# dt and u in the order of the units: one 512 KB spread with 4 KB pieces in place of two with 2 KB pieces

## The chip, the cores and the metric

The kernel runs on one core of a Trainium2 chip, in one launch. The metric is the device time of that launch in microseconds (us); lower is better. A core has TensorE (PE; its weight loads are listed as PEld), VectorE (DVE), ScalarE (ACT), GpSimd (POOL) and SyncE (SP), which run their own instruction streams and wait for each other on semaphores, and 16 DMA engines that move data between the memories. In this kernel SP alone issues DMAs.

## The reference

A layer over an input of 8 x 512 x 256: causal latent attention with 16 heads, a feed-forward part with blockwise 4-bit rounding, a two-directional state-space model, and the feed-forward part again, each with a residual. The change is in the state-space model. For each of the 8 batch elements and 2 directions it computes, with 512 channels, 16 states and 512 time steps:

```
dt  = softplus(dt @ dt_w + dt_b)                    # 512 steps x 512 channels
dA  = exp(dt[..., None] * A)                        # A: 512 channels x 16 states
dBu = dt[..., None] * B_ssm[:, :, None, :] * xc[..., None]
def step(h, inp):
    dAt, dBut, ct = inp
    h = dAt * h + dBut
    return h, einsum('bdn,bn->bd', h, ct)
y = scan(step, 0, (dA, dBu, C_ssm)) + xc * D_skip
```

u is dt * xc; dBu is u times the row of B of each state.

## The kernel before

**Blocks, groups, units.** Each batch element is a block of 64 units, numbered K = 0 to 511 over the kernel (NU = 64, NK = 512). A group g is 128 channels in one direction; a block has 8 groups, and a group has 8 units (q = 0 to 7). A unit is 16 channels with all 16 states, as two halves e = 0 and 1 of 8 channels x 16 states = 128 partitions x 512 steps.

**A unit's work.** ACT makes the factors dA of both halves (`factors`, L1355) into two PSUM banks; POOL makes dBu of both halves in one instruction (`make_dBu`, L1074); DVE scans each half (L943) and multiplies it by C (L950); PE sums the states of two units at a time (`state_sum`, L1657). There is one pair of factor banks, so ACT waits for DVE's L950 of the unit before. dBu has four slots; the dBu of unit K+2 stands before unit K's other work on POOL, and waits until the pair before it was summed. In the last block the odd units from k = 15 (`shared`) have their second half multiplied by POOL (L1081).

**How dt and u come to 128 partitions.** dt and u of a group are 128 channels x 512 steps in SBUF. SP stores each to DRAM (`store_dt`, `store_u`: `kept_dt[g]`, `kept_u[g]`, 128 rows of 2 KB), and for each unit loads the 8 rows of a half, repeated for the 16 states, to 128 partitions: a spread of 256 KB, twice for a unit and tensor (`spread_dt`, L581; `spread_u`, L572). The rows of a half are

```
def row_block(q, e):
    return QG * ((2 * q + e) % QG) + q // 2        # QG = 4
r = CT * row_block(q, e)                           # CT = 8
return kept[r:r + CT].unsqueeze(0).to_broadcast([DS, CT, T])
```

so the two halves of a unit lie 32 rows apart. u has two buffers (US = 2), dt has three (RS = 3).

**The order on SP.** In unit K the queue has: the spread of dt for K+3 (after dA of K), the spread of u for K+4 (after dBu of K+2), behind q = 0 the load of the next xc, behind q = 3 the stores of the next group's dt and u, behind q = 6 the load of the next dt input, and four units before a new direction the rows of B and C (`load_states`, L588 and L592). The first spread of a group waits for that group's store (L577, L568). A waiting instruction holds all that stands behind it on SP.

**The side work.** Between the units each engine does visits of the work beside: the merge, the output and the second feed-forward part of the block before (`merge`, 18 visits, and `ffn`, 47), and latents (26), attention (65), the first feed-forward part (47) and the preparation (`prep`, 27) of the block after. How many visits stand at each half unit is written out by hand in `VISITS`, one base-36 digit for each half unit, and all engines follow the same table: "first" for block 0, "middle" for blocks 1 to 6, "last" for block 7.

## Time and profile before

| | us |
|---|---|
| median of 3 runs (3790.64 to 3798.03) | 3791.13 |
| profiled execution, its own time | 3796.87 |
| its span | 3795.1 |
| DVE busy | 3057.4 |
| PE busy | 2855.8 |
| ACT, POOL busy | 1991.5, 1949.1 |

The profiled execution's time is 1.8 us more than its span, and 5.7 us above the median. The span divides into about 317 us ahead of the first unit, 402 us for block 0, about 442 us for each of the blocks 1 to 6, 331 us for block 7 and 93 us behind the last unit. The busy shares are means over stretches that are limited by different things, so they say little of themselves: it has to be read where an engine is nearly always busy, and what it waits for where it is not.

### The profile page before, as it was taken

The page shows a single profiled execution, that of the slowest core. Times are in us where ns is not written, and L with a number is a line of the kernel's source. Part 1 is how long each engine was busy: PE and PEld are TensorE (multiplying, and loading weights), DVE is VectorE, ACT ScalarE, POOL GpSimd, SP SyncE. Part 2 cuts the span into 40 slices and gives each one's busy share as a digit, 9 for nine tenths or more (in the row PEclk, how much of TensorE's full clock was granted, in tenths as well). Part 3 has the DMA queues.
Part 4 walks back from the last instruction along what each step waited for, and adds up shares of the span by engine and source line. Part 5 has one row for each costly group of instructions (what it writes and reads, how often), then busy time and mean ns, then how long its engine had stood idle before and what let it go on. Part 6 is the DMA issues. An engine that isn't in the chain of part 4 may idle for free.

```text
span 3795.1 us, 41535 instructions
## 1 busy us (share of the span) xinstructions
PE 2855.8 (75%) x12965; PEld 1467.3 (39%) x12965; DVE 3057.4 (81%) x4262; ACT 1991.5 (52%) x3811; POOL 1949.1 (51%) x1115
## 2 busy tenths in 40 slices
PE   7963877689776987679776897769866797765436
PEld 3631444245423553245442454235532454422103
DVE  5354889797988989788897979888897888979765
ACT  2533665446653575546654466535755466544332
POOL 2014754556545654447545565456544475456671
PEclk9976988899987998799988999879987999887657
DMA  3007885966668665867759666786658677597890
GB/s 94 1 17 209 212 221 159 273 159 179 175 205 240 174 179 152 252 166 193 206 150 272 160 177 175 204 240 175 180 153 247 168 192 208 144 269 209 233 246 19
DMA packets 373277, 691.40 MB, mean 182 GB/s; under 512 B 52157, under 2 KB 63552, under 8 KB 366912
## 3 DMA queue, kind: packets, MB, share of 16 engines
q1 hardware_dynamic: 373056, 688.74, 67.3%
q8 instruction: 104, 1.70, 0.2%
q14 instruction: 117, 0.96, 0.1%
HBM read 603.65 MB, written 84.93 MB: 181 GB/s over the span
## 4 chain that ended last, share of the span: by engine, by line
PE 42%; DVE 27%; ACT 9%; issue 7%; POOL 7%; DMA 6%; SPq 1%; POOLq 0%; ACTq 0%; DVEq 0%
PE banks L1387 22%; DVE banks L943 7%; PE banks L1579 5%; PE banks L1392 5%; POOL sb_arena L1074 4%; DVE sb_arena L950 4%; PE banks L1657 4%; PE banks L1555 3%; ACT banks L1355 3%; ACT sb_arena L1121 2%; DMA sb_arena<-kept_u 2%; PE banks L1427 2%; DVE sb_arena L652 2%; PE banks L1401 2%; DVE sb_arena L847 2%
## 5 line engine op out<-in xcount | busy, mean ns | idle before, releaser
L1074 POOL TENSOR_TENSOR sb_arena<-sb_arena 128x1024 f32<-128x1024 f32 x512 | 1205.6, 2359 | 970.3 <-PE banks L1657 605.5
L943 DVE TENSOR_TENSOR_SCAN banks<-banks,sb_arena 128x512 f32<-128x512 f32 x999 | 1171.4, 1217 | 277.0 <-ACT banks L1355 203.5
L1355 ACT ACTIVATE banks<-sb_arena,sb_neg_a 128x512 f32<-128x512 f32 x1024 | 665.1, 682 | 982.8 <-DVE sb_arena L950 792.0
L1657 PE MATMUL banks<-sb_arena,sb_w_sum 128*32 128x512 f32 x2048 | 336.5, 729 | 461.7 <-DVE sb_arena L950 363.4
L950 DVE TENSOR_TENSOR sb_arena<-banks,sb_arena 128x512 f32<-128x512 f32 x999 | 636.8, 678 | 0.0
L1392 PE MATMUL banks<-sb_ident,sb_arena 128*128 128x128 f32 (+1 forms) x2083 | 358.5, 296 | 364.3 <-POOL sb_arena L984 153.2
L1121 ACT ACTIVATE sb_arena<-banks 128x512 f32<-128x512 f32 (+2 forms) x720 | 360.6, 517 | 510.7 <-PE banks L1392 344.8
L1392 PEld LDWEIGHTS banks<-sb_ident,sb_arena 128*128 128x128 f32 (+1 forms) x2083 | 242.4, 148 | 575.0 <-ACT sb_arena L1121 224.4
L801 DVE TENSOR_REDUCE sb_nmax<-banks 128x1 f32<-128x512 f32 (+3 forms) x352 | 222.7, 635 | 187.0 <-PE banks L1582 186.5
L1387 PE MATMUL banks<-sb_w_gu,sb_arena 128*128 128x352 f32 x1024 | 362.5, 505 | 5.5 <-ACT sb_arena L1121 5.5
L1579 PE MATMUL banks<-sb_arena 128*128 128x384 f32 (+3 forms) x1024 | 361.1, 464 | 4.5 <-POOL sb_arena L1001 4.5
L1657 PEld LDWEIGHTS banks<-sb_arena,sb_w_sum 128*32 128x32 f32 x2048 | 46.0, 117 | 633.1 <-DVE sb_arena L950 443.6
L991 POOL TENSOR_TENSOR sb_arena<-sb_arena,sb_q_s 128x704 f32<-128x704 f32 x64 | 88.7, 1386 | 377.1 <-DVE sb_arena L670 367.5
L1197 ACT ACTIVATE sb_arena<-banks,sb_nmax 128x512 f32<-128x512 f32 (+3 forms) x512 | 266.2, 536 | 26.4 <-DVE sb_nmax L801 25.7
L1387 PEld LDWEIGHTS banks<-sb_w_gu,sb_arena 128*128 128x128 f32 x1024 | 209.0, 212 | 119.9 <-issue 31.5
L1387 PE MATMUL banks<-sb_arena,sb_w_lat 128*128 128x512 f32 x512 | 233.8, 607 | 13.3 <-DVE sb_arena L788 8.2
L1427 PE MATMUL banks<-sb_arena,sb_w_merge 128*128 128x512 f32 x448 | 215.4, 640 | 0.0
L1401 PE MATMUL banks<-sb_identb,sb_zerob 128*128 128x512 bf16 x640 | 215.1, 411 | 0.0
L1387 PE MATMUL banks<-sb_w_down,sb_arena 128*128 128x256 f32 (+1 forms) x768 | 205.1, 412 | 9.6 <-ACT sb_arena L1121 7.8
L1555 PE MATMUL banks<-sb_arena 128*32 128x128 f32 x2560 | 185.9, 280 | 1.9 <-ACT sb_arena L1121 1.9
L1387 PE MATMUL banks<-sb_arena,sb_w_in 128*128 128x512 f32 x256 | 151.0, 725 | 47.8 <-DVE sb_arena L847 46.9
L1579 PEld LDWEIGHTS banks<-sb_arena 128*128 128x128 f32 x1024 | 156.0, 194 | 66.4 <-issue 43.3
(132 smaller groups left out, 4020.9 us busy)
## 6 DMA issues: line engine op xcount, KB each, us to landing
sb_arena<-kept_dt SPq DMA_DIRECT2D x1024, 256.0 KB, 5.2
sb_arena<-kept_u SPq DMA_DIRECT2D x1024, 256.0 KB, 4.6
kept_xc<-sb_arena SPq DMA_DIRECT2D x16, 1024.0 KB, 4.9
kept_z<-sb_arena SPq DMA_DIRECT2D x16, 1024.0 KB, 5.5
sb_arena<-kept_xc SPq DMA_DIRECT2D x64, 256.0 KB, 5.6
kept_dt<-sb_arena SPq DMA_DIRECT2D x64, 256.0 KB, 3.9
kept_u<-sb_arena SPq DMA_DIRECT2D x64, 256.0 KB, 3.9
sb_arena<-kept_z SPq DMA_DIRECT2D x63, 256.0 KB, 5.8
```

The costliest lines, as they stand in the source:

```text
L943: v.tensor_tensor_scan(products if e == 1 and shared(K) else factors, factors, products, 0.0, ALU.mult, ALU.add).then_inc(V.sem, V.mark("s ...
L950: v.tensor_tensor(dBu[K % SLOTS][:, e], psum[:, e], ct[:, gd % 2], ALU.mult).then_inc(V.sem, V.mark("hc", K, e))
L1074: nc.gpsimd.tensor_tensor(dBu[K % SLOTS], rows_u[K % US], bt[:, gd % 2].unsqueeze(1).to_broadcast([P, 2, T]), ALU.mult).then_inc(G.sem, G. ...
L1121: nc.scalar.activation(dst, src, ACT.Copy).then_inc(A.sem, A.mark(*name))
L1355: nc.scalar.activation(psum[:, e], rows_dt[K % RS][:, e], ACT.Exp, scale=neg_a[:, s, m, j:j + 1]).then_inc(A.sem, A.mark("dA", K, e))
L1387: mm = pe.matmul(dst, lhs, rhs, start=(i == 0), stop=(i == len(pairs) - 1))
L1392: mm = pe.transpose(dst, src, ident[0:src.shape[0], 0:src.shape[0]])
L1401: pe.matmul(psum[:, YB], zerob[:, :], identb[:, :].unsqueeze(1).to_broadcast([P, T // P, P]), start=False, stop=False)
L1427: mm = pe.matmul(psum[:, SB[j]], w_merge[:, k, j * P:j * P + P], ycat[:, k], start=(k == 0), stop=(k == 2 * DT - 1))
L1555: mm = pe.matmul(psum[L * r:L * r + L, SB[4], m * P:m * P + P], val[:, at:at + L], prT[:, slot, c * P:c * P + P], start=(k == 0), stop=(k ...
L1579: pe.matmul(psum[:, bank, e * kl:e * kl + kl], qz[:, m, r], lat[1][:, m, 0:kl], start=(e == 0), stop=False)
L1657: mm = pe.matmul(psum[r:r + L, YB], w_sum[:, L * o:L * o + L], dBu[k % SLOTS][:, e], start=(o == 0), stop=(o == QG - 1))
```

## The change

The two DRAM tensors get the shape (group, unit of the group, channel of the half, half, step): 16 rows of 2 KB of one unit lie together, and a channel's two halves are 4 KB in a row. Each group's store is cut by blocks of 32 partitions, four for dt and four for u, each writing 32 pieces of 2 KB. Each unit's spread is one DMA for both halves. The counts in the waits follow. `VISITS` has other numbers; the visits in sum, and the instructions of PE, DVE, ACT and POOL, are the same.

```
@@ VISITS (of three tables, the first row of "middle") @@
-    "middle": "0012003103011116093755733052020212123201040107405110222120313130"
+    "middle": "1112010202101035082933111352315112022111201302010323102032211031"
...
-        kept_dt, kept_u = scratch("kept_dt", (NG, P, T)), scratch("kept_u", (NG, P, T))
+        kept_dt, kept_u = scratch("kept_dt", (NG, NQ, CT, 2, T)), scratch("kept_u", (NG, NQ, CT, 2, T))
...
             def store_u(g):
                 sp.wait_ge(G.sem, G.at("u", g))
-                sp.dma_start(kept_u[g], u).then_inc(s_kept_u, 16)
+                for r in range(QG):
+                    sp.dma_start(blocks_of(kept_u[g], r), u[L * r:L * r + L]).then_inc(s_kept_u, 16)
+
+            def blocks_of(kept, r):
+
+                return kept[r // 2::2, :, r % 2]
+
+            def over_states(kept, q):
+
+                return kept[q].rearrange("c e t -> c (e t)").unsqueeze(0).to_broadcast([DS, CT, 2 * T])
 
             def spread_u(K):
                 g, q = divmod(K, NQ)
                 if q == 0:
-                    sp.wait_ge(s_kept_u, 16 * (g + 1))
+                    sp.wait_ge(s_kept_u, 16 * QG * (g + 1))
                 if K >= US:
                     sp.wait_ge(G.sem, G.at("dBu", K - US))
-                for e in range(2):
-                    sp.dma_start(rows_u[K % US][:, e], over_states(kept_u[g], q, e)).then_inc(s_u[K % US], 16)
+                sp.dma_start(rows_u[K % US].rearrange("p e t -> p (e t)"), over_states(kept_u[g], q)
+                             ).then_inc(s_u[K % US], 16)
```

`store_dt` and `spread_dt` change in the same way.

How SP's queue changes is seen at a store, here that of the second group (the names: `kept_dt` and `kept_u` are the DRAM tensors, `sb_arena` holds the buffers). Before:

```order
L581 DMA sb_arena<-kept_dt 128x1x512 x2
L572 DMA sb_arena<-kept_u 128x1x512 x2
L554 DMA kept_dt<-sb_arena 128x512
L558 DMA kept_u<-sb_arena 128x512
L581 DMA sb_arena<-kept_dt 128x1x512 x2
L572 DMA sb_arena<-kept_u 128x1x512 x2
```

And now:

```order
L585 DMA sb_arena<-kept_dt 128x1x1024
L576 DMA sb_arena<-kept_u 128x1x1024
L555 DMA kept_dt<-sb_arena 4x8x512 x4
L560 DMA kept_u<-sb_arena 4x8x512 x4
L585 DMA sb_arena<-kept_dt 128x1x1024
L576 DMA sb_arena<-kept_u 128x1x1024
```

A spread went from two issues to one, a pair of stores from two issues to eight, and the DRAM side of a store now has an outer dimension of 4.

What the table moves is seen on DVE in block 3, at the units k = 33 to 35, which lie in attention (L801, now L806, is attention's maximum; L943 and L950, now L948 and L955, are a unit's scan and its product with C). Before:

```order
L943 SCALAR_TENSOR_TENSOR banks<-banks,sb_arena 128x512 x2
L801 TENSOR_REDUCE sb_nmax<-banks 128x1
L950 TENSOR_TENSOR sb_arena<-banks,sb_arena 128x512 x2
L943 SCALAR_TENSOR_TENSOR banks<-banks,sb_arena 128x512 x2
L801 TENSOR_REDUCE sb_nmax<-banks 128x1
L950 TENSOR_TENSOR sb_arena<-banks,sb_arena 128x512 x2
L943 SCALAR_TENSOR_TENSOR banks<-banks,sb_arena 128x512 x2
L807 TENSOR_TENSOR sb_arena<-sb_arena,banks 128x512
L801 TENSOR_REDUCE sb_nmax<-banks 128x1
L950 TENSOR_TENSOR sb_arena<-banks,sb_arena 128x512 x2
```

And now:

```order
L948 SCALAR_TENSOR_TENSOR banks<-banks,sb_arena 128x512 x2
L806 TENSOR_REDUCE sb_nmax<-banks 128x1
L955 TENSOR_TENSOR sb_arena<-banks,sb_arena 128x512 x2
L817 TENSOR_TENSOR sb_x<-sb_xin,banks 128x256
L806 TENSOR_REDUCE sb_nmax<-banks 128x1
L678 BN_STATS sb_stats<-sb_x 128x6
L806 TENSOR_REDUCE sb_nmax<-banks 128x1 x5
L948 SCALAR_TENSOR_TENSOR banks<-banks,sb_arena 128x512 x2
L806 TENSOR_REDUCE sb_nmax<-banks 128x1 x3
L826 RECIPROCAL sb_einv<-sb_esum 128x16
L806 TENSOR_REDUCE sb_nmax<-banks 128x1 x5
L955 TENSOR_TENSOR sb_arena<-banks,sb_arena 128x512 x2
```

Attention's steps were spread over the units one at a time; now more than a dozen of them stand within two units, and fewer units stand between attention's beginning and its end (16.5 in place of 19 in a middle block, counted from the tables).

## Rows read from the trace of the kernel before

**Rows 1.** The page: shares of the chain that ended last, by engine.

```profile
PE 42%; DVE 27%; ACT 9%; issue 7%; POOL 7%; DMA 6%; SPq 1%; POOLq 0%; ACTq 0%; DVEq 0%
```

**Rows 2.** Stretches: us; PE, PEld, DVE, ACT, POOL busy; PEclk, DMA share, GB/s.

```profile
1603.00:1627.00 24.00, 20.97 (x50) 8.42 (x50) 18.86 (x30) 9.34 (x15) 13.15 (x7) 0.93 1.07 272
...
1645.00:1705.00 60.00, 44.81 (x174) 26.83 (x172) 53.83 (x86) 28.32 (x42) 25.45 (x17) 0.89 0.44 119
...
1744.00:1775.00 31.00, 30.40 (x181) 18.81 (x179) 22.40 (x30) 19.88 (x66) 24.32 (x13) 1.00 0.72 184
...
2010.00:2027.00 17.00, 4.42 (x20) 0.61 (x18) 14.37 (x18) 9.53 (x17) 9.65 (x6) 0.67 1.03 278
2027.00:2047.00 20.00, 7.04 (x26) 1.40 (x27) 14.47 (x17) 5.42 (x9) 12.80 (x7) 0.50 0.98 283
```

**Rows 3.** The chain, start us, us, what: the edge between blocks 4 and 5.

```profile
2460.49 5.53 DMA sb_arena<-kept_u
...
2476.40 4.90 DMA kept_u<-sb_arena
...
2481.87 0.60 SPq L572
...
2482.57 4.13 DMA sb_arena<-rows_bc
...
2499.20 0.60 SPq L572
...
2500.73 7.67 DMA sb_arena<-kept_zs
```

**Rows 4.** The timeline of that edge: in brackets the engine's idle time and its releaser.

```profile
2490.10 1.30 ACT L1355 ACTIVATE banks<-sb_arena,sb_neg_a 128x512 f32<-128x512 f32 x2 [6.00 <-DMA sb_arena<-kept_dt]
...
2490.89 2.35 DVE L943 TENSOR_TENSOR_SCAN banks<-banks,sb_arena 128x512 f32<-128x512 f32 x2 [3.78 <-ACT banks L1355]
...
2493.15 1.27 DVE L950 TENSOR_TENSOR sb_arena<-banks,sb_arena 128x512 f32<-128x512 f32 x2
```

**Rows 5.** The timeline in block 7, two units, POOL and PE.

```profile
3603.11 2.34 POOL L1074 TENSOR_TENSOR sb_arena<-sb_arena 128x1024 f32<-128x1024 f32 x1 [1.79 <-DMA sb_arena<-kept_u]
...
3606.73 1.94 PE L1657 MATMUL banks<-sb_arena,sb_w_sum 128*32 128x512 f32 x8 [7.76 <-POOL sb_arena L1081]
...
3608.84 2.35 POOL L1074 TENSOR_TENSOR sb_arena<-sb_arena 128x1024 f32<-128x1024 f32 x1 [2.17 <-PE banks L1657]
...
3612.07 2.35 POOL L1074 TENSOR_TENSOR sb_arena<-sb_arena 128x1024 f32<-128x1024 f32 x1 [0.88 <-DMA sb_arena<-kept_u]
...
3614.38 1.26 POOL L1081 TENSOR_TENSOR sb_arena<-sb_arena 128x512 f32<-128x512 f32 x1
...
3617.84 2.35 POOL L1074 TENSOR_TENSOR sb_arena<-sb_arena 128x1024 f32<-128x1024 f32 x1 [2.21 <-PE banks L1657]
```

**Rows 6.** A stretch of block 7, columns as in rows 2.

```profile
3561.00:3668.00 107.00, 36.31 (x113) 8.30 (x113) 72.85 (x80) 40.60 (x64) 77.70 (x45) 0.60 0.94 245
```

**Rows 7.** SP's issues of a spread of u: ns min/median/max.

```profile
L572 SPq DMA_DIRECT2D sb_arena<-kept_u x1024: 514/597/1460, 321.4 to 3699.2; - x171
```

**Rows 8.** The same of the store of u, and its landing.

```profile
L558 SPq DMA_DIRECT2D kept_u<-sb_arena x64: 325/430/1357, 316.0 to 3666.7; - x64
...
DMA to landing us min/median/max: 2.0/3.9/7.3
```

**Rows 9.** SP's waits: for what, us in total, times, longest.

```profile
SPq L572 <- DMA kept_u<-sb_arena: 71.1, 33, 4.8
```

**Rows 10.** The DMA queue: packets, MB, packets' time as a share of 16 engines' span.

```profile
q1 hardware_dynamic: 373056, 688.74, 67.3%
```

**Rows 11.** Stretches as in rows 2: weights; spreads of dt alone; spreads of dt and u.

```profile
26.00:30.00 4.00, 3.15 (x10) 2.26 (x11) 3.69 (x7) 1.19 (x2) 0.00 (x0) 0.50 0.90 340
...
316.00:320.00 4.00, 0.00 (x0) 0.00 (x0) 0.00 (x0) 1.30 (x2) 0.00 (x0) 0.50 1.07 247
...
1130.00:1135.00 5.00, 0.94 (x8) 0.23 (x8) 3.91 (x5) 4.35 (x9) 2.36 (x2) 0.68 1.02 329
```

30 lines of the change are left out of this document (14 added, 16 removed).

## The prediction

> **What bounds the kernel now.** I read the chain that ended last first. DMA is 6% of it and SP's queue 1%, against 42% for PE and 27% for DVE [rows 1]: of 3795.1 us some 228 us hang on a transfer, and the change touches no instruction of an engine. So I asked where in a block the DMA part lies, by cutting a middle block into stretches [rows 2]. The second feed-forward part (1645 to 1705) has DVE busy 53.8 us of 60 at a DMA share of 0.44: DVE's own. Attention (1744 to 1775) has PE busy 30.4 of 31: PE's own. At the edge between two blocks (2010 to 2047, and 1603 to 1627 behind the edge before) there is little side work, units follow each other fast, the DMA share is 0.98 to 1.07 at 272 to 283 GB/s, and DVE is busy 14.4 of 17, 14.5 of 20 and 18.9 of 24 us. Here transfers decide. The chain at an edge shows which [rows 3]: a spread of u (5.53 us), the store of u (4.90), the second issue of a spread (0.60), the rows of B and C (4.13), another second issue (0.60), and the load of the gate `kept_zs` (7.67), which is queued behind spreads. The 4.90 us of the store hold SP, behind it stands the spread of dt, and so ACT waits 6.00 us and DVE 3.78 us [rows 4]. There are 7 such edges (in front of blocks 1 to 7). The second place is block 7 from about unit 24 on, with almost no side work: a share of 0.94, DVE busy 72.9 of 107 us [rows 6]. Two units there take 9.0 us (3608.84 to 3617.84), in a ring of POOL's dBu, a wait for the spread of u (0.88 here, 1.79 two units before), dBu again, POOL's product (1.26), PE's sum (1.94) and the next dBu [rows 5].
>
> **Part 1, one issue in place of two.** An issue of a spread takes SP 0.597 us (median) [rows 7], and POOL and ACT wait for both halves, so the second half starts 0.6 us late. In block 7 this 0.6 us lies ahead of the wait for u in each pair of units; the wait (0.88 and 1.79) is longer, so it goes through: 20 pairs x 0.6 = 12 us. At an edge the chain holds a second issue twice in so many words, and once more inside the spread it begins with: 3 x 0.6 x 7 = 12.6 us. I assume that the one issue takes no longer than one of the two did, since it has as many pieces (128); if it took twice as long, this part would be 0, and that is the bound on the other side. Elsewhere it is worth nothing: DVE or PE is busy, and the spreads are two or three units ahead.
>
> **Part 2, pieces of 4 KB.** The bytes stay the same. The trace has no repeated load with 4 KB pieces, so I bound it by rates. Weights, each row read once, arrive at 340 GB/s; spreads, whose rows are read 16 times, ran at 247 GB/s at one place and 329 at another [rows 11], and 272 to 283 at the edges. If what slows them is the repeated reading, longer pieces change nothing: 0. If it is the piece, they could come up to 340, 18% less time than at 280. The three edge stretches are 61 us, of which DVE is idle 13.3 us; some 12 units pass in them and I leave 0.3 us between ACT and DVE in each, so at most 9.7 us can go, 68 us over 7 edges. In block 7 the ring without the wait for u is 2 x 2.35 + 1.26 + 1.94 + some 0.3 = 8.2 us against 9.0, so at most 0.8 x 20 = 16 us, of which part 1 has taken 12. I take 7% for the speed, nearer to 0, because both 247 and 329 were reached with the same pieces and so the piece is not the whole reason: 7% of 61 us is 4.3, of which 2.5 us fall where DVE is idle; 7 x 2.5 = 17.5, and 2.5 in block 7: 20 us.
>
> One rule speaks against even that. The rates of rows 11 differ by a third at the same piece size. The Trainium skill ("DMA: Bandwidth & Descriptors", section "Why small descriptors are slow (HBM only)") puts a fixed cost of about three cycles on each packet, beside a cycle for each 32 bytes: for 2 KB that would be under 5%, and half of it saved, some 2%. By it part 2 would be about 6 us in place of 20.
>
> **Part 3, eight stores in place of two.** This is what the change pays with. Before, the store of u takes 0.43 us to issue and lands 3.9 us later (medians) [rows 8]. In half of the groups SP then waits for it: 33 times, 71.1 us in all [rows 9]. Now six more issues at 0.43 stand ahead of the last landing: +2.6 us, the lower bound. The upper bound comes from the shape that the order shows, 4x8x512 on the DRAM side: if a transfer is divided among the DMA engines by its outer dimension, all 512 KB of a group's dt and u go through 4 engines in place of 16. A busy engine moves 688.74 MB / (0.673 x 16 x 3795.1 us) = 16.9 KB per us [rows 10], so 128 KB take 7.8 us in place of 1.9: +5.8 us. I take +3.2, near the lower bound, since no row shows such a division. At the 7 edges the wait has no slack: SP's next spreads, the rows of B and C and ACT's factors all stand behind it [rows 3, 4]: 7 x 3.2 = 22.4 us. In block 7's last four groups units are as fast, and about 1.2 us of slack remain behind POOL's other work (an estimate: PE's sum holds the dBu as often as the spread does, rows 5): 4 x 2.0 = 8 us. In the other groups units take 7 us and more, and the spread is used many us after it lands: nothing; the cover is the side work, and if the table took it away there, each would cost up to 3.2 as well. The SP queue itself gains: 16 issues fewer for spreads in a group, 6 more for stores.
>
> A rule of the skill goes with the upper bound. No transfer here with an outer dimension under 16 has a landing of its own in the rows, so no run so far shows it. The Trainium skill (the same page, section "Why a DMA increments its semaphore by 16 and not by 1") says that the number of engines is the largest up to 16 that divides the slowest dimension of both sides; that would be 4 here. By it part 3 is 7 x 5.8 + 4 x 4.6 = 59 us in place of 30.
>
> **Part 4, the table.** The visits are as many as before; in a middle block the second feed-forward part is spread over 7.5 units in place of 5.5, attention over 16.5 in place of 19. A light unit costs DVE 3.6 us (2.35 + 1.27 of scan and product [rows 4]). Two more units beside the feed-forward part, where DVE is idle 6.2 of 60 us, could cost 2 x 3.6 = 7.3 us less what fits in the idle time; 2.5 units fewer beside attention, where PE leaves no room, could give back 0 to 9 us. So a middle block may change by -9 to +7 us, and six of them by -54 to +42. The signs cancel on the rows that I have; I take 0.
>
> **The sum.** -12 - 12.6 - 20 + 22.4 + 8 + 0 = -14 us, from 3796.87 us of the profiled execution to 3783. That execution was 5.7 us above the median of the runs shown; taken from the median, 3791.1 - 14 = 3777, say 3776.
>
> **Rivals.**
> (a) The stores win: they run on a quarter of the engines, the u store lands 5.8 us later, and the spreads gain only their second issue (25 us). 59 - 25 = +34, less up to 10 from pieces: 3815 to 3825, slower. It decides from the point at which the stores cost more than the spreads gain: with gains of 25 us that is a store of u that lands some 2.7 us later (7 x 2.7 + 4 x 1.5 = 25), with gains of 45 one that lands 4.5 us later. For it: the shape, and the 6.00 us wait that already hangs on this store. Against: nothing in the trace shows the division.
> (b) Nothing moves: spreads and stores cancel, or the 0.6 us are taken up by the next wait (PE's sum behind POOL's product, 2.2 us in rows 5): 3784 to 3799. For it: DMA is 6% of the chain only.
> (c) The pieces are the reason for the slow spreads: gains of 25 + 60, stores 30: 3736 to 3760. For it: 340 against 280 GB/s. Against: 329 with 2 KB pieces.
> (d) The table alone decides, by more than 10 us in either direction: 3745 or 3815. For it: every middle block is the same, so 2 us in one are 12 in all.
>
> **How the numbers follow.** The forecast (gains a little above the stores; 3763 to 3783) has 0.35; (c) 0.12; (b) 0.2; (a) 0.18; (d) 0.15, split 0.07 faster and 0.08 slower. A measurement tells a change of about 0.2%, 7.6 us, from none. Faster: 0.35 + 0.12 + 0.07, less a little for the forecast's upper part = 0.52; within 0.2%: 0.2; slower: 0.18 + 0.08 and that little = 0.28. The range leaves out 0.1 below (the best of (c) with a table that helps) and 0.1 above (the full 59 us with no gain): 3736 to 3822.
>
> **What would show it.** Part 1: the issue of a spread at 0.6 us with 512 KB, SP's issue time halved. Part 2: the GB/s at a share near 1.0 at the edges, above or at 280; the u spread's landing. Part 3: the landing of the last store of u behind the first issue of the group (before 3.9 + 0.6), SP's wait for it (71.1 us in 33), and ACT's wait for dt at the edge (6.00). Part 4: the length of a middle block, 442 us, with the edges taken out. I would be wrong by most if blocks 1 to 6 changed in their middles, or if the store of u landed 6 us later.

## The result, and the profile after

The changed kernel takes 3992.89 us in the median (3989.61 to 3997.83) against 3790.89 us for the kernel before beside it on the same chip: a ratio of 1.0531, interval 1.0512 to 1.055, or 202 us slower. The prediction was 3776 us, and its range ended at 3822.

The page of the changed kernel begins with these rows: the span; the chain that ended last by engine (rows 1 of before); the DMA queue (rows 10); and the issues of spreads and stores, with their size and the median time to landing.

```profile
span 3996.0 us, 40839 instructions
...
PE 31%; DVE 28%; POOL 12%; issue 10%; DMA 10%; ACT 6%; SPq 2%; POOLq 0%; ACTq 0%; DVEq 0%
...
q1 hardware_dynamic: 225600, 688.68, 67.6%
...
sb_arena<-kept_dt SPq DMA_DIRECT2D x512, 512.0 KB, 7.3
sb_arena<-kept_u SPq DMA_DIRECT2D x512, 512.0 KB, 6.4
```

DMA is 10% of the chain where it was 6%, and POOL 12% where it was 7%. The same bytes took the same share of a longer span. Worked out as in the prediction's part 3, a busy DMA engine moved 688.68 MB / (0.676 x 16 x 3996.0 us) = 15.9 KB per us, where it had been 16.9. I call this figure **the rate of a busy engine** from here on. It is a mean over all transfers of the program, of which the spreads are some 78% (537 of 689 MB), and the packets' times can overlap (a share of 1.07 in rows 11), so it serves for comparing these kernels and is no engine's true speed.

SP's waits, and the waits of POOL and ACT for spreads, in us in total, times and longest:

```profile
SPq L576 <- DMA kept_u<-sb_arena: 157.3, 44, 6.5
```

```profile
POOL sb_arena L1079 <- DMA sb_arena<-kept_u: 498.2, 175, 19.4
ACT banks L1360 <- DMA sb_arena<-kept_dt: 398.8, 91, 13.6
```

The first answers to rows 9 (71.1 us in 33). Of before, POOL's wait for u was 324.4 us and ACT's for dt 190.3: the two waits grew by 382 us together (they overlap in part, so this is not time of the kernel).

The issue of a spread of u (L576) and of a store of u (L560), ns min/median/max; they answer to rows 7 and 8:

```profile
L576 SPq DMA_DIRECT2D sb_arena<-kept_u x512: 514/515/1901, 326.0 to 3902.0; - x171
```

```profile
L560 SPq DMA_DIRECT2D kept_u<-sb_arena x256: 579/582/637, 316.5 to 3868.2; - x128
```

The single issue is indeed no longer than one of the two was (515 against 597 ns). But a store now takes 0.58 us, more than the 0.43 us of the 256 KB store of before.

The chain at the edge between blocks 4 and 5 (rows 3), start us, us, what; first two lines of before, then the changed kernel:

```profile
2474.50 1.27 POOL sb_arena L1065
2475.77 0.58 SPq L554
```

```profile
2589.63 1.28 POOL sb_arena L1070
...
2590.96 0.63 SPq L555
...
2594.13 0.58 SPq L560
...
2594.76 7.68 DMA kept_u<-sb_arena
2602.43 0.02 issue
2602.45 0.56 SPq L576
...
2603.11 5.17 DMA sb_arena<-rows_bc
...
2608.44 2.34 POOL sb_arena L1079
...
2617.16 9.13 DMA sb_arena<-kept_zs
```

From POOL's end (2590.91) to the landing of the store (2602.43) it is 11.5 us; of before it was 5.5 us (from 2475.77 to 2481.3, the end of the store in rows 3). Behind it B and C take 5.17 us in place of 4.13, and the gate 9.13 in place of 7.67. ACT's timeline there answers to rows 4:

```profile
2603.70 1.30 ACT L1360 ACTIVATE banks<-sb_arena,sb_neg_a 128x512 f32<-128x512 f32 x2 [6.33 <-DMA sb_arena<-kept_dt]
2611.68 1.30 ACT L1360 ACTIVATE banks<-sb_arena,sb_neg_a 128x512 f32<-128x512 f32 x2 [6.68 <-DMA sb_arena<-kept_dt]
2616.22 1.30 ACT L1360 ACTIVATE banks<-sb_arena,sb_neg_a 128x512 f32<-128x512 f32 x2 [3.24 <-DMA sb_arena<-kept_dt]
```

Of before, beside the 6.00 us of rows 4, the units ahead of it and behind it waited too:

```profile
2482.80 1.30 ACT L1355 ACTIVATE banks<-sb_arena,sb_neg_a 128x512 f32<-128x512 f32 x2 [2.74 <-DMA sb_arena<-kept_dt]
2494.10 1.30 ACT L1355 ACTIVATE banks<-sb_arena,sb_neg_a 128x512 f32<-128x512 f32 x2 [2.70 <-DMA sb_arena<-kept_dt]
```

So three units in a row wait for dt in both kernels, 11.4 us together before and 16.3 us now. Stretches of the span (columns as in rows 2): the last eight units of block 3, and units 32 to 53 of block 7, in the kernel before:

```profile
2009.60:2046.70 37.10, 11.55 (x46) 1.87 (x45) 29.25 (x34) 15.05 (x25) 22.86 (x12) 0.58 1.00 280
3561.60:3667.30 105.70, 36.17 (x113) 8.30 (x113) 72.85 (x80) 39.90 (x63) 77.31 (x44) 0.60 0.93 245
```

And the same units now:

```profile
2095.70:2139.10 43.40, 10.70 (x44) 1.83 (x43) 29.23 (x34) 16.11 (x26) 21.32 (x11) 0.56 0.91 237
3749.60:3866.10 116.50, 36.04 (x112) 8.61 (x112) 72.83 (x80) 39.76 (x62) 77.85 (x45) 0.59 0.93 222
```

DVE does the same work in both (29.2 and 72.8 us). The last eight units have become 43.4 us from 37.1, and the 22 units of block 7 116.5 us from 105.7, with the DMA engines as busy as before in block 7 (0.93) and moving less (222 GB/s in place of 245). In that stretch ACT's waits for dt grew most, from 21.4 us to 58.7, and POOL's for u from 11.5 us in 7 waits to 25.1 in 8. One of them, where rows 5 had 0.88 and 1.79:

```profile
3789.94 2.34 POOL L1079 TENSOR_TENSOR sb_arena<-sb_arena 128x1024 f32<-128x1024 f32 x1 [4.70 <-DMA sb_arena<-kept_u]
```

All in all a middle block went from 443 us to 469, block 0 from 402 to 419 and block 7 from 331 to 361 (from the start of a block's first factors to that of the next one's; block 7 to the start of its last unit's). So the middles of blocks changed too, which the prediction had named as its worst case.

### The profile page after: what moved, and what is told of

Its sections match the earlier page's. It is cut to its first block, busy times and chain, and to the rows that moved or that the text cites. A ratio compares the mean times of both kernels' runs of the same rounds, so it can differ in the third digit from the quotient of the medians.

```text
span 3996.0 us, 40839 instructions
## 1 busy us (share of the span) xinstructions
PE 2887.9 (72%) x12937; PEld 1483.6 (37%) x12937; DVE 3106.3 (78%) x4262; ACT 1991.3 (50%) x3811; POOL 1954.8 (49%) x1115
## 3 DMA queue, kind: packets, MB, share of 16 engines
q1 hardware_dynamic: 225600, 688.68, 67.6%
## 4 chain that ended last, share of the span: by engine, by line
PE 31%; DVE 28%; POOL 12%; issue 10%; DMA 10%; ACT 6%; SPq 2%; POOLq 0%; ACTq 0%; DVEq 0%
PE banks L1392 13%; DVE banks L948 8%; POOL sb_arena L1079 7%; PE banks L1584 6%; DMA sb_arena<-kept_u 5%; PE banks L1397 4%; DVE sb_arena L955 4%; PE banks L1662 3%; PE banks L1560 3%; DMA kept_u<-sb_arena 2%; DVE sb_arena L657 2%; ACT banks L1360 2%; DVE sb_arena L662 2%; DVE sb_arena L667 2%; DVE sb_arena L671 2%
## 5 line engine op out<-in xcount | busy, mean ns | idle before, releaser
L948 DVE TENSOR_TENSOR_SCAN banks<-banks,sb_arena 128x512 f32<-128x512 f32 x999 | 1170.6, 1216 | 355.8 <-ACT banks L1360 286.6
L955 DVE TENSOR_TENSOR sb_arena<-banks,sb_arena 128x512 f32<-128x512 f32 x999 | 636.3, 677 | 0.0
L806 DVE TENSOR_REDUCE sb_nmax<-banks 128x1 f32<-128x512 f32 (+3 forms) x352 | 223.8, 637 | 253.8 <-PE banks L1587 253.4
L1584 PE MATMUL banks<-sb_arena 128*128 128x384 f32 (+3 forms) x1024 | 371.0, 478 | 26.2 <-POOL sb_arena L1006 20.5
L1392 PE MATMUL banks<-sb_w_down,sb_arena 128*128 128x256 f32 (+1 forms) x768 | 233.6, 455 | 76.1 <-ACT sb_arena L1126 74.4
L1202 ACT ACTIVATE sb_arena<-banks,sb_nmax 128x512 f32<-128x512 f32 (+3 forms) x512 | 265.1, 526 | 29.2 <-DVE sb_nmax L806 28.3
L1392 PEld LDWEIGHTS banks<-sb_w_down,sb_arena 128*128 128x128 f32 (+1 forms) x768 | 161.6, 224 | 149.8 <-ACT sb_arena L1126 101.6
L1406 PE MATMUL banks<-sb_identb,sb_zerob 128*128 128x512 bf16 x612 | 202.0, 407 | 0.0
L1584 PEld LDWEIGHTS banks<-sb_arena 128*128 128x128 f32 x1024 | 166.7, 207 | 85.0 <-issue 39.4
```

Of the source, the lines that this page charges most:

```text
L806: v.tensor_reduce(nmax[:, at:at + ne], psum[:, bank, 0:ne * kl].rearrange("p (e k) -> p e k", k=kl), AX.X, ALU.max, negate=True).then_inc( ...
L948: v.tensor_tensor_scan(products if e == 1 and shared(K) else factors, factors, products, 0.0, ALU.mult, ALU.add).then_inc(V.sem, V.mark("s ...
L955: v.tensor_tensor(dBu[K % SLOTS][:, e], psum[:, e], ct[:, gd % 2], ALU.mult).then_inc(V.sem, V.mark("hc", K, e))
L1202: nc.scalar.activation(pr[:, slot, e * kl:e * kl + kl], psum[:, SB[j % 3], e * kl:e * kl + kl], ACT.Exp, bias=nmax[:, c:c + 1], accum_out= ...
L1392: mm = pe.matmul(dst, lhs, rhs, start=(i == 0), stop=(i == len(pairs) - 1))
L1584: pe.matmul(psum[:, bank, e * kl:e * kl + kl], qz[:, m, r], lat[1][:, m, 0:kl], start=(e == 0), stop=False)
```

## The experiments

All are compared with the kernel before in the same job (medians 3790.0 to 3792.2 us); "+8 us" is the difference of the two medians.

### One part at a time

**e1, the table alone.** The kernel before with the changed kernel's `VISITS`.

> The kernel before with the new tables and nothing else. Theory T (the table is the cause of the loss: a middle block's units k = 32 to 39 went from 41 to 68 us, while the spread itself did not change): 3930 to 3990 us. Theory S (stores and spreads are the cause, the table costs nothing of its own): 3780 to 3805 us. If both share it: some 3850 to 3900.

3856.02 us, ratio 1.017 (1.0152 to 1.0189): **+64 us**. Middle blocks take 451 to 455 us, some 11 more; block 0 and block 7, whose tables changed as well, stayed within 1 us. The loss is not at the edges but in units 16 to 39, which take 159 us in place of 152, and in units 40 to 47, 77 in place of 73. Units 16 to 47 of block 3, in the kernel before and in e1:

```profile
1720.90:1946.60 225.70, 196.11 (x1096) 109.26 (x1095) 195.56 (x273) 139.67 (x304) 129.35 (x73) 0.96 0.68 175
```

```profile
1739.40:1975.80 236.40, 201.12 (x1101) 110.64 (x1099) 199.97 (x272) 139.74 (x303) 128.50 (x73) 0.96 0.64 171
```

PE is busy 5.0 us more and idle 5.7 us more (means over the six middle blocks: 5.8 and 5.2). The work came in from units 8 to 15, which give 5 of their visits to units 16 to 39: the stretch above holds 12 matmuls of the latents more (64 for 52, 29.1 us for 23.3). Units 8 to 15 of block 3, before and in e1:

```profile
1644.80:1720.90 76.10, 59.25 (x238) 34.12 (x236) 69.27 (x105) 37.51 (x58) 34.81 (x22) 0.91 0.50 135
```

```profile
1664.80:1739.40 74.60, 54.06 (x219) 31.16 (x218) 69.90 (x102) 36.30 (x56) 35.25 (x21) 0.89 0.51 135
```

PE was rid of 5.2 us there, and the units became only 1.5 us shorter, because DVE, busy 69.9 of 74.6 us, is what fills them. The idle time lies between a thin strip, in which PE has 109 matmuls in 40 us (units 16 to 23), and a crowded one with 432 in 68 us (units 32 to 39).

**e8, the new table for units 8 to 39 of the middle blocks alone.** `"middle"` with the new digits at those half units only.

> The kernel before with the new digits of the table of visits for the middle blocks' units 8 to 39 alone (first and last block, and units 0 to 7 and 40 to 63, as before). In e1 (the whole new table, +64 us) a middle block was 442 -> 454 us, and its units 8 to 40 alone some +6 us. Theory M (the loss sits where attention now meets fewer units, and it adds up block by block): 6 x 5 to 7 = +30 to +45 us here, and the other 20 to 30 us of e1 lie in units 40 to 63 and in the first block. Rival F (the first and the last block's table, or the feed-forward part at an edge, make the loss): under +15 us here.

3823.3 us, ratio 1.009 (1.0072 to 1.0109): **+33 us**, half of e1's. Theory M holds. The middle blocks came to 447 to 453 us; blocks 0 and 7, whose tables are as before, were 6 and 4 us shorter in the profiled execution. Units 16 to 39 take the same 159 us as in e1; the rest of e1's loss lies mainly in the units behind (units 40 to 47 took 77.0 us in e1 and 72.9 here). Units 16 to 47 of block 3:

```profile
1727.70:1959.60 231.90, 200.70 (x1113) 110.89 (x1112) 196.58 (x274) 140.46 (x307) 128.73 (x73) 0.96 0.65 171
```

Against before (225.7 us, PE busy 196.1) PE is busy 4.6 us more and idle 1.6 us more; over the six middle blocks it is 5.7 and 1.1. So the half of the loss that e8 has is nearly all work of PE that was moved into its full stretch, and most of the idle time comes with the digits behind unit 39.

**e2, the layout alone** (the changed kernel with the old table).

> The changed kernel with the tables of before: layout, eight stores and single spreads alone. Theory S: 3930 to 3990 us, the whole loss. Theory T: within 20 us of 3791. If the two parts add up, this one's difference from before and that of the tables alone sum to 202 us.

3905.95 us, ratio 1.0297 (1.0278 to 1.0315): **+114 us**. Table and layout are both losses by themselves, and make 178 of the 202 us.

**e3, the layout with stores over 16 engines.** As e2, but an order whose slowest dimension in a store is 32 channels:

```
- kept_dt, kept_u = scratch("kept_dt", (NG, NQ, CT, 2, T)), ...
+ kept_dt, kept_u = scratch("kept_dt", (NG, 2, NQ // 2, CT, 2, T)), ...
- return kept[r // 2::2, :, r % 2]                                    # 4 x 8 x 512
+ return kept[r // 2].rearrange("o c e t -> (o c) e t")[:, r % 2]     # 32 x 512
```

> As the kernel with the new layout and the old tables, but the units of a group lie in the order of (q % 2, q // 2), so that the DRAM side of each of the eight stores is 32 rows with one step (32x512 in place of 4x8x512); bytes, pieces, number of issues and the single 512 KB spreads are the same. Theory S4 (a store with an outer dimension of 4 runs on few DMA engines and lands late): the time falls by more than half of what the layout alone costs, and the wait of SP for the store of u falls from 157 us to near the 71 us of before. Theory P (the single spread with 4 KB pieces is what costs): within 15 us of the layout alone.

3838.71 us, ratio 1.012 (1.0098 to 1.0142): **+46.5 us**. The stores' shape cost e2 67 us.

**e4, the changed kernel's stores alone** (spreads in two transfers of 2 KB pieces, old table).

> The eight stores in the new layout (4x8x512), with the tables of before and the spreads of before: two issues of 256 KB in 2 KB pieces for a unit. Theory S4: nearly as slow as the kernel with the whole new layout, at least 3791 + 59 x 0.7 = 3830 us by the price of rival (a). Theory P: 3785 to 3810 us.

3851.04 us, ratio 1.0155 (1.014 to 1.0171): **+59 us**, the very price that the prediction gave to four engines, but not made up as it had it. SP's queue at the edge between blocks 4 and 5:

```profile
2508.42 2.57 SPq L555 DMA_DIRECT2D kept_dt<-sb_arena  x4
2511.03 2.46 SPq L560 DMA_DIRECT2D kept_u<-sb_arena  x4
2513.53 1.22 SPq L586 DMA_DIRECT2D sb_arena<-kept_dt  x2
2517.87 1.16 SPq L577 DMA_DIRECT2D sb_arena<-kept_u  x2
```

The first spread of u waits for the last store: 9.4 us from the first issue, where it was 5.5 (2475.77 to 2481.3). Over the seven edges the means are 9.1 and 5.6 us, so the store lands 3.5 us later, not the 5.8 of the upper bound.

**e5, eight stores over 16 engines alone** (e3's stores, before's spreads and table).

> The kernel before with eight stores per group of 32 rows x 512 channels-columns in place of two (dt and u in an order that has 32 as the slowest dimension), the old table, and the spreads as before: two transfers of 256 KB with 2 KB pieces per unit and array. It differs from e3 in the spreads alone and from e4 in the shape of the stores alone. Theory S (the single 512 KB transfer is what costs in e3): e3 was +46.5 us, and eight issues of 0.43 us cost only what they delay, 2.6 us at 7 edges and little else: +10 to +22 us here, so that the single spread takes 25 to 36 us of e3. Rival R (the issues of the stores cost, the spreads nothing): +40 to +50 us here. The same run against e4 (+59) gives the price of the outer dimension 4: 37 to 49 us by S, 10 to 20 us by R. The wait for the store of u (71.1 us in 33 before, 64.2 us in 35 in e3, 94.9 in 44 in e4) should be some 70 to 90 us in both.

3800.46 us, ratio 1.0022 (1.0011 to 1.0033): **+10 us**. Theory S holds, and more: SP hardly waits for these stores any more.

```profile
SPq L577 <- DMA kept_u<-sb_arena: 11.7, 12, 3.0
```

Its edge between blocks 4 and 5, in the chain:

```profile
2478.92 0.58 SPq L555
...
2480.97 0.42 SPq L560
...
2482.36 1.78 DMA kept_u<-sb_arena
```

From the first issue to the landing it is 5.2 us, no more than the 5.5 us of before (over the seven edges 5.8 and 5.6): the first stores land while the later ones are being issued, and each is a quarter as long. Two differences follow. Stores over four engines cost e4 - e5 = **49 us** over stores of the same number, size and bytes over 16. The single spread costs e3 - e5 = **36.5 us**, where the prediction had it gain 45.

That the stores do run on four engines is seen in the packet counts too. e3 and e2 differ by 231744 - 225600 = 6144 packets in q1, e5 and e4 by 379200 - 373056 = 6144: for 512 stores that is 12 small packets each, as it would be if 4 engines reported each store's end in place of 16. The Trainium skill's rule that the number of engines is the largest up to 16 that divides the slowest dimension of both sides ("DMA: Bandwidth & Descriptors", "Why a DMA increments its semaphore by 16 and not by 1") agrees with this and with the 49 and 67 us.

### The spread: issue, piece, or rows

The next kernels have the table of before and its two stores to a group, and each changes only where `spread_u` and `spread_dt` read and how they are cut (e13 and e14 also where the stores write). In each but e13, some partitions get other channels than they should; bytes and the work of the engines are the same. That an engine takes an equal share of a transfer's outermost dimension, one after the other, is an assumption here; no trace tells which engine read which row.

**e6, a row for each DMA engine.** `kept[16*q:16*q+16].unsqueeze(1).to_broadcast([16, 8, T])` for both halves.

> The kernel before with another source for the spreads: each half takes 16 rows of dt (or u), each repeated 8 times, in place of 8 rows repeated 16 times, so half of the channels and states are paired otherwise and the values are not the reference's; bytes, pieces (2 KB), issues, and the number of instructions on every engine are the same. A transfer is now divided over its 16 rows, so each DMA engine reads one row of its own, 8 times, in place of all 16 engines reading the same 8 rows. Theory H (engines that read the same row at the same time slow each other): a packet of a spread falls from 123 ns toward 84 ns, the landing of u from 5.4 to under 4.8 us, and the time by 30 to 100 us (3690 to 3760 us), since the edges and block 7 hang on transfers. Rival B (a repeated 2 KB read costs what it costs, wherever it comes from, or the limit is on the writing side): packets 115 to 125 ns, time within 10 us of before.

3791.06 us, ratio 1.0004 (0.9994 to 1.0015): **no change**. Theory H's 30 to 100 us did not come. But e6 doesn't only take away that 16 engines read the same row, it also has each engine read one row 8 times in a row, which the kernel before doesn't; that one of these was exchanged for the other isn't excluded by this run.

**e9, two issues with 4 KB pieces** (64 partitions each, 16 rows of 4 KB repeated 4 times).

> The kernel before (its two stores, its table) with another source and another cut for the spreads: two transfers of 256 KB per unit and array as before, but each covers 64 partitions with both halves, 64 pieces of 4 KB in place of 128 of 2 KB; the rows are 16 of the stored array, each repeated 4 times, so the values are not the reference's. It differs from e6 (two issues, 2 KB, no change in the time) in the size of the pieces alone. Theory Q (the longer piece is what e3's spreads lost 38 us by against e5's): packets of 4 KB at about 269 ns against 2 x 122, +25 to +45 us. Rival O (the one issue in place of two is what costs, since nothing is seen before the whole has landed): packets under 250 ns and -10 to +10 us here.

3818.51 us, ratio 1.0072 (1.0056 to 1.0089): **+27 us**. The number of issues is the same as before, so the pieces cost (or the cut over 64 partitions, which e11 does without and loses more).

**e11, one issue with 4 KB pieces** (16 rows, 8 times).

> The kernel before (its two stores, its table) with one transfer of 512 KB per unit and array in pieces of 4 KB, as the changed kernel has it, but over 16 rows that are each repeated 8 times, so the values are not the reference's. With e6 (two issues, 2 KB), e9 (two, 4 KB) and e10 (one, 2 KB) it makes the fourth corner, with the stores and the table of before in all. If the cost of e3's spreads (38 us against e5) lies in the spread alone and not in its meeting the eight stores: +30 to +46 us, and e9 and e10 together make up about this one. Rival (the cost needs the eight stores beside it, or the eight rows that all engines read together): under +15 us.

3837.86 us, ratio 1.0129 (1.0112 to 1.0146): **+46 us**, all of e3's loss, without the eight stores and without eight rows that all engines share. The expectation's other half, that e9 and e10 together make up this one, failed: 27 - 73.5 is not +46, since e10 changes the rows too.

**e10, one issue with 2 KB pieces** (each partition its own stored row, twice).

```
- for e in range(2):
-     sp.dma_start(rows_u[K % US][:, e], over_states(kept_u[g], q, e)).then_inc(s_u[K % US], 16)
+ sp.dma_start(rows_u[K % US], kept_u[g].unsqueeze(1).to_broadcast([P, 2, T])).then_inc(s_u[K % US], 16)
```

> The kernel before (its two stores, its table) with one transfer of 512 KB per unit and array in pieces of 2 KB: each partition takes its own stored row twice, so the values are not the reference's. It differs from e6 in the number of issues (and in how often a row is read). Theory Q (the longer piece costs): -12 to +8 us, since an issue is saved and the pieces are the same; packets about 122 ns. Rival O (the one issue costs): +25 to +45 us.

3718.02 us, ratio 0.9813 (0.9797 to 0.9828): **-73.5 us**. Neither theory had this: the saved issue was to give 12 us at most. The other thing that e10 changes is how many different rows a transfer reads, 128 in place of 16.

**e12, two issues over 128 rows.** Before's two transfers, with `over_states` returning all of `kept`.

> The kernel before with another source for the spreads: two transfers of 256 KB per unit and array as before, each over all 128 stored rows (256 KB of memory), one row to a partition, so the values are not the reference's. It differs from e10 (one issue of the same rows and pieces, -73 us, packets of 84 ns in the median) in the number of issues alone, and from e6 (16 rows within 32 KB, repeated 8 times, no change) in the rows alone. Theory M (16 engines that read within the same 16 to 64 KB of memory slow each other, rows far apart do not): packets of 84 to 98 ns and -50 to -70 us; what is left to e10 is the issue that is saved, 5 to 20 us. Rival I (it is the single issue with 2 KB pieces that gains, a 2 KB row costs the same wherever it lies): -10 to +5 us and packets near 120 ns.

3728.92 us, ratio 0.9829 (0.9806 to 0.9851): **-62 us**, with before's issues and before's pieces. So the rows make it; the issue that e10 saves is worth the 11 us between them, if that much (the intervals overlap).

**e15, one issue with 4 KB pieces over 64 rows**, each twice.

> e11 (one transfer of 512 KB in 4 KB pieces, +46 us) with 64 different rows of 4 KB, each read twice, in place of 16 rows read 8 times; not the reference's values. It differs from e10 (-73 us) in the length of the piece alone, and from e11 in the rows alone. If the piece costs by itself: well behind e10, -40 us or less gained. If the 4 KB piece only makes a crowded place more crowded: packets of 160 to 190 ns and within 10 us of e10 (3710 to 3730 us).

3728.05 us, ratio 0.9828 (0.981 to 0.9845): **-63 us**. The longer piece costs little or nothing here, where it cost 46 us in e11. It costs where the rows are few.

**e13 and e14, the same few rows 130 KB apart.** `kept_dt` and `kept_u` as `(P, NG + 1, T)`, read and written as `[:, g]`; e13 with the spreads of before, e14 with e6's.

> The kernel before with dt and u stored row by row far apart: row r of group g at (65 r + g) x 2 KB, so the 8 rows of a spread lie 130 KB from each other in place of 2 KB; everything else as before, and the values are the reference's. Theory M1 (what counts is how far apart the places are that are read at a time): packets fall toward 84 to 100 ns and the time by 40 to 70 us. Theory M2 (what counts is that the 16 engines read the same row at the same time, which they still do here): -10 to +10 us. A version that could beat both kernels.

> The source of e6 (16 rows, each repeated 8 times, a row to each DMA engine; not the reference's values) with the rows 130 KB apart as in e13. No two engines read the same row and no two rows are neighbours. By M1: 40 to 70 us faster, like e13. By M2: e6 already had a row for each engine and gained nothing (0), so M2 needs both, own rows and rows apart: 40 to 70 us faster here, none in e13. If the repeating itself (a row 8 times by one engine) is what costs: within 10 us of before here and in e13, against -50 or more in e12.

3790.19 us, ratio 1.0 (0.9991 to 1.001), and 3782.39 us, 0.9976 (0.9965 to 0.9988): **-1 and -9 us**. Where the rows lie matters hardly, M1 fell, and of M2's 40 to 70 us there are 9. The third account that stands in e14's expectation, that a row read 8 times by one engine costs by itself, named what came: within 10 us of before in both, and -50 or more in e12.

**e16, 32 rows, each 4 times**, two issues with 2 KB pieces.

> The kernel before with another source for the spreads: two transfers of 256 KB in pieces of 2 KB, each over 32 stored rows that are repeated 4 times; not the reference's values. Between e12 (128 rows once, packets of 84 ns in the median, -62 us) and e6 (16 rows 8 times, 121 ns, no change). Theory G (the more often a transfer reads the same row, the slower each reading, by degrees): 90 to 110 ns in the median and -20 to -50 us. Rival E (twice is still free, as e10 and e15 showed, and from some number on it costs the whole): under 90 ns and -50 to -65 us, or 118 ns and over and -5 to +5 us.

3738.21 us, ratio 0.986 (0.9833 to 0.9886): **-52 us**. Rival E, or near it: between 16 rows and 32 lies nearly the whole difference.

The rows of q1 in five of these (e11, e6, e16, e12, e15 in this order; packets, MB, share of 16 engines):

```profile
q1 hardware_dynamic: 225600, 688.68, 70.8%
```

```profile
q1 hardware_dynamic: 373056, 688.74, 66.5%
```

```profile
q1 hardware_dynamic: 373056, 688.74, 55.0%
```

```profile
q1 hardware_dynamic: 373056, 688.74, 55.6%
```

```profile
q1 hardware_dynamic: 225600, 688.68, 54.4%
```

With their spans (3844.5, 3789.2, 3731.0, 3727.9, 3725.4 us) they give the rate of a busy engine, and so for all:

| | issues, piece | different rows in a transfer | KB per us of a busy engine | us |
|---|---|---|---|---|
| before, e13 | 2, 2 KB | 8 | 16.9, 16.7 | 0, -1 |
| e6, e14 | 2, 2 KB | 16 | 17.1, 17.7 | 0, -9 |
| e9 | 2, 4 KB | 16 | 16.4 | +27 |
| e11 | 1, 4 KB | 16 | 15.8 | +46 |
| e3 (with 8 stores) | 1, 4 KB | 8 | 15.7 | +46.5 |
| e16 | 2, 2 KB | 32 | 21.0 | -52 |
| e12 | 2, 2 KB | 128 | 20.8 | -62 |
| e10 | 1, 2 KB | 128 | 20.9 | -73.5 |
| e15 | 1, 4 KB | 64 | 21.2 | -63 |

With 16 rows or fewer an engine moves 15.7 to 17.7 KB per us, with 32 or more 20.8 to 21.2. (The weights of rows 11 came at 340 GB/s with a share of 0.90, so by the same measure at 23.6.) How many different bytes a unit reads doesn't order the table: e11 and e16 both read 64 KB of dt for a unit, at 15.8 and 21.0. Another account fits most of the table: how often in a row one engine reads the same row again (8 times and more in e6 and, over its two transfers, in e9, up to 4 in e16). The kernel before, whose engines each go through 8 rows, and is slow nonetheless, speaks against taking that account alone; there, by the assumption above, all 16 engines read the same row at about the same time, so the two could be slow for different reasons. I leave it open. A single transfer with 2 KB pieces over the 8 right rows was not tried; it needs a pattern of four dimensions.

The Trainium skill gives as a rule to prefer one transfer over 128 partitions to two over halves (the same page, "Rules for kernel authors"). Here two transfers over halves were faster than one: e9 at +27 against e11 at +46, with the same pieces and rows. Where the rows are many, one transfer was no slower than two (e10 and e12, whose two are not halves of the partitions). The measurement decides: under this repeated reading the rule doesn't hold.

### Table and layout together

**e17, e3 with the new table.**

> e3 (eight stores over 16 engines, single spreads with 4 KB pieces; +46 us with the old table) with the new table of visits, or the changed kernel with its stores over 16 engines. The changed kernel is at +202 us, while table alone (+64) and layout alone (+114) make 178. If the 24 us between are the four-engine stores' (in the new table their waits are less covered): the sum holds here, +46 + 64 = +110 us, 3901 us, and the changed kernel lies 92 us behind this. If they are the spreads': +125 to +135 us here, and the changed kernel lies 67 to 77 us behind.

3912.47 us, ratio 1.0313 (1.0293 to 1.0334): **+122 us**, 12 more than the sum of e3 and e1; and the changed kernel, which differs from it in the stores' shape, lies 80 us behind, 12 more than e2 behind e3. The 24 us are shared between spreads and stores. They lie in units 16 to 39 of the middle blocks: against before these 24 units, six blocks together, take 43 us more in e1 and 8 more in e2, but 78 more in the changed kernel. The prediction had named this way in its part 3 (the cover is the side work, and the table could take it away), and put no price on it in the sum.

### Could the right values have the gain?

e12 gains because it reads other rows than it should. A kernel with the right values has another way: to need fewer bytes.

**e7, 16 channels x 8 states on the partitions.** The halves are halves of the states, both use the same spread, and a unit needs one transfer of 256 KB of dt and one of u. The zero matmuls that fill PE's gaps during a sum are left out:

```
- for e in range(2):
-     sp.dma_start(rows_u[K % US][:, e], over_states(kept_u[g], q, e)).then_inc(s_u[K % US], 16)
+ sp.dma_start(rows_u[K % US], over_states(kept_u[g], q)).then_inc(s_u[K % US], 16)
...
- r = L * ((2 * k + e) % QG)
- mm = pe.matmul(psum[r:r + L, YB], w_sum[:, L * o:L * o + L], dBu[k % SLOTS][:, e], ...)
+ mm = pe.matmul(psum[L * o:L * o + L, YB], w_sum[:, L * (k % 2):L * (k % 2) + L], dBu[k % SLOTS][:, e], ...)
```

> The kernel before with another assignment of channels and states to the 128 partitions: 16 channels x 8 states, and the two halves of a unit are the two halves of the states. Both halves then use the same rows of dt and u, so a unit needs one spread of 256 KB of each in place of two; B and C are spread in two transfers each per block. The old table; the zero matmuls that keep PE busy during a sum are left out. Spreads move 344 MB in place of 688 MB. Theory T (edges and block 7 hang on the volume of the spreads): the DMA share in them falls from about 1.0 to about 0.55, the edges lose 5 to 12 us each and block 7 10 to 25 us: 3640 to 3745 us. Rival N (the stores, POOL and DVE hold the edges, and the rate is not what counts): 3770 to 3800 us. Rival P (the sum without its filling lets the clock of PE fall): PE's matmuls elsewhere get slower and the time is above 3800 us with a lower granted clock in the middle blocks.

4165.68 us, ratio 1.0987 (1.0971 to 1.1003): **+375 us**, outside of all three (the time would fit rival P, but the granted clock rose, 0.91 against 0.87). ACT's wait for dt fell to 55.4 us as hoped, but the sums on PE (count | busy us, mean ns of one) went from 336.5 us to:

```profile
L1659 PE MATMUL banks<-sb_arena,sb_w_sum 128*32 128x512 f32 x2048 | 1026.7, 650 | 350.8 <-DVE sb_arena L954 232.2
```

A matmul is no longer (650 ns against 729), but in the kernel before the four of a pair go to four strips of 32 output rows and overlap: 2048 x 729 ns = 1493 us of matmuls in 336.5 us. In e7 all four go to one strip.

**e18, e7 with the pair on two strips.** Channels are dealt so that units k and k+1 go to strips of their own, `r = L * (k % QG)`, and the four matmuls alternate; the filling is back in one of its four gaps.

> e7 (16 channels x 8 states on the partitions, one spread of 256 KB per unit and array, half the bytes of before; +375 us) with the channels dealt to the strips of PE's output otherwise: the four matmuls that sum a pair of units went to one strip of 32 output rows in e7, now to two strips in turn; the kernel before sends them to four. The filling matmuls run in one of four gaps. In e7 the sums kept PE busy 1026.7 us where before it was 336.5, and the waits for spreads had all but gone (ACT 55.4 us for kept_dt). Theory P (e7 lost by the sums alone, since matmuls to one strip don't overlap): sums at 550 to 700 us busy, e7's loss at least halved: 3850 to 3980 us. If the gain from half the bytes (45 to 80 us, as much as e12 gave) then outweighs what the sums still cost: 3750 to 3800 us. Rival W (e7's loss is elsewhere, in the waits of POOL or the clock): 4100 us or more, whatever the strips.

3838.06 us, ratio 1.0131 (1.0114 to 1.0148): **+48 us**, with the sums at

```profile
L1662 PE MATMUL banks<-sb_arena,sb_w_sum 128*32 128x512 f32 x2048 | 601.6, 717 | 365.7 <-DVE sb_arena L955 278.5
```

327 of e7's 375 us lay in that strip, a little more than theory P's range asked. At the edges e18 is faster than before (the last and first 8 units of blocks take about 34 + 40 us in place of 37 + 42), but units 16 to 31, where PE is nearly always busy, take 116.3 us in place of 110.6, and block 7 takes 344 in place of 331. There the longer sums cost more than the transfers give back. No kernel that I ran with the reference's values beats the kernel before.

## Why the prediction was wrong, point by point

Taken apart by the runs, the 202 us are: eight issues +10 (e5), four engines in place of 16 +49 (e4 - e5), the single spread +36.5 (e3 - e5), stores and spreads together +18 more than apart (e2), the table +64 (e1), and table with layout +24. The prediction's sum had -14.

**What bounds the kernel: right.** Edges and the end of block 7 hang on transfers. e12, which only makes the transfers faster, gains 62 us, all but a few at those places: a block's last and first 8 units take 34 + 37 us in place of 37 + 42, block 7 takes 318.5 us in place of 331.4, and the 48 units between differ by 1 us a block.

**Part 1, one issue in place of two (-24.6): the duration right, the gain mis-sized.** The issue took 515 ns, as assumed. The wait for u that the sum charged in each of 20 pairs of units of block 7 was there less often: in 22 units of the kernel before POOL waits for u 7 times, 11.5 us in all. The gain was at most 11 us where transfers were fast (e10 against e12). With 16 rows and 4 KB pieces it was a loss of 19 us (e11 against e9). That nothing of a longer transfer can be used before its end is not the reason: in e9 too POOL and ACT wait for both transfers. What the pages show is a rate of 15.8 against 16.4 KB per us, and that a store of u, the same in both, lands 4.8 us after its issue in place of 4.0. Why a single issue does this stays open.

**Part 2, 4 KB pieces (-20, bounds 0 to -84): wrong in its sign.** Parts 1 and 2 together were -44.6 in the sum, and the single spread with 4 KB pieces measured +36.5. I had bounded it by 0, since "if what slows them is the repeated reading, longer pieces change nothing". The premise was right and what I drew from it wrong: what slows spreads is the repeated reading of few rows (e16, e12), and under it longer pieces are slower still, 15.8 against 17.1 KB per us (e11, e6). I had no row that excluded a loss, and should have let the bound go above 0. The observation that 247 and 329 GB/s were reached with the same pieces pointed at a cause outside of the piece. I used it to shrink the gain and did not ask what the cause would make of the new shape.

**Part 3, the stores (+30, bounds about +24 to +59): on four engines, as the upper bound had it, and priced right by luck there.** The stores alone cost 59 us (e4), which is what four engines gave in the sum. But in e4 the store lands 3.5 us later at the edges, not 5.8, close to the 3.2 that I took. The edges became 33 us longer (the last and first 8 units around each, 4.8 us for each edge) and block 7's last 40 units 12.5, 46 us in place of the 59, and some 17 us more lie where the sum had nothing: in block 0 and in units 16 to 55 of the middle blocks. So two errors met: a delay too long by the bound, and no cost in the other groups. In the changed kernel the landing at the edge shown is 6.0 us later, because the single spreads stand ahead as well (over the seven edges 11.4 us from the first issue, against 9.1 in e4). I had written "no row shows such a division", but no row spoke against it either, and the shape 4x8x512 stood in the order: where a structural reason names one end and nothing names the other, the middle is not the cautious value. The lower bound was wrong the other way. Eight issues over 16 engines do not delay the landing by 2.6 us, but by 0.2 (5.8 us against 5.6), and cost 10 us, not 24.

**Part 4, the table (0, bounds -54 to +42): outside its bounds.** +64 us: each middle block got 11 us longer, where I had +7 at most. I had priced units moved toward the feed-forward part by DVE's light unit, and given attention "0 to 9 us back" for its 2.5 units fewer. The runs show the reverse: units 8 to 15, beside the feed-forward part, got 1.2 us shorter, and units 16 to 47 got 11 us longer. Of these, 5.8 us are work of PE that came in from units 8 to 15, where it had fitted beside DVE's, and 5.2 us are idle time of PE (e1). 33 of the 64 us come with the table of units 8 to 39 alone, and there it is nearly all such work (e8). The missing term is how many matmuls the table moves into the stretch that PE fills: it can be counted before any run.

**The rivals.** (a) had four engines for the stores and, by luck, their price, but credited 25 us and up to 10 more for spreads, which turned out a cost of 36.5. (d) had a table that counts, at 24 us. That stores, spreads and table are losses at once was in none: I had let each of the others be a gain or nothing in every rival, so the range ended at 3822 where the sum of the upper ends, with a spread that may lose, would have been about 3900 (an estimate: 3791 + 59 + 42 = 3892, and what the spread loses). The interactions of 42 us lie beyond even that.

## What to carry to other kernels

Before making the pieces of a broadcast load longer, look at how many different rows a transfer reads: the rate of a busy engine, bytes over share, engines and span, tells from one page whether the engines run at the faster or the slower of the two rates seen here, and at the slower one longer pieces made it worse. A store whose slowest dimension is 4 ran on 4 engines here; splitting it the same way with 32 outermost costs a sixth of it here (10 us against 59). And a table that was tuned to one kernel has to be priced as a change of its own: here it was a third of the loss. Count first what it moves into the stretch where an engine is nearly always busy: that work costs its full length, while the stretch that it leaves gets hardly shorter if another engine fills it.

## What the hardware showed that I had not expected

- Transfers that read 8 or 16 different rows over and over run at 15.7 to 17.7 KB per us and engine, those over 32 to 128 rows at 20.8 to 21.2, and giving each engine rows of its own, or laying the rows 130 KB apart, or both, changed the time by 0, -1 and -9 us (e6, e13, e14). The cause stays open.
- Under that load 4 KB pieces are slower per byte than 2 KB ones (15.8 and 16.4 against 17.1); without it they are not (21.2 against 20.9).
- SP takes 0.58 us to issue a 64 KB store that goes over four engines, and 0.42 us over 16 (e4, e5).
- Four matmuls with 32 output columns to four strips took 336.5 us in all, to two strips 601.6, to one 1026.7, at 650 to 730 ns each. The Trainium skill tells of such tiles working in parallel ("TensorEngine Tiling (Array Packing)", "Key Properties"), and the trace agrees.
